# Expert tiles whose normalized rows pass through a DRAM scratch and are turned by VectorE, in place of 16 TensorE transposes per tile

## The chip, the cores and the metric

The kernel runs on one core of one Trainium2 chip. The metric is the device time of one execution in microseconds (us); the kernel before takes 2157.5 us, the median of three runs (2156.28 to 2159.11). Engines are TensorE (PE; PEld is its weight load), VectorE (DVE), ScalarE (ACT), GpSimd (POOL) and SyncE (SP), which in this kernel issues every DMA. The profile was taken of one execution.

## The reference, cut to what matters

The input `x` is (8, 512, 2048) in float32: 4096 tokens of 2048 features. The first half of the reference is an autocorrelation attention over `ctx_4096`; its result is added to `x`. The change does not touch it. The second half is a feed-forward layer of gated low-rank experts:

```python
    x = x + _L0_xattn_ref(_layernorm(x, axis=-1), ctx_4096, ctx_4096)
    x = x + _L0_ffn_ref(_layernorm(x, axis=-1), A_w, B_w, Wq_w, keys)

    # _L0_ffn_ref(x, A_w (512, 2048), B_w (2048, 512), Wq_w (16, 2048), keys (64, 16))
    q = jnp.einsum('bsd,rd->bsr', x, Wq_w)
    scores = jnp.einsum('bsr,er->bse', q, keys)
    top_vals, top_idx = jax.lax.top_k(scores, 16)
    top_w = jax.nn.softmax(top_vals, axis=-1)
    gate = jnp.sum(one_hot(top_idx, 64) * top_w[..., None], axis=-2)
    z = jnp.einsum('bsd,nd->bsn', x, A_w).reshape(..., 64, 8)
    z_gated = (z * gate[..., None]).reshape(..., 512)
    out = jnp.einsum('bsn,on->bso', z_gated, B_w) * 2.0
```

## The kernel before

The first part (to about 1350 us) runs 32 attention groups and writes their result to the output tensor in DRAM. The second part takes the 4096 tokens in 32 tiles of 128 tokens, one after another; `TT` is 32. Only this second part is changed, and mostly its tiles 4 to 31.

`each_tile` calls a function `tile_step(u, ...)` on every engine for u = 0 to 32. Step u does the products of tile u (`a`), adds the output of tile u-1 (`b`), prepares tile u+1 (`f`) and loads and sums tile u+2 (`later_tile(u)`). Steps 5 to 28 are a loop. The order of the instructions of an engine is the order in which they are written out in its `tile_step`; an engine that waits on a semaphore holds up all that stands behind it, and so does SP for the DMAs that it issues. There are four row buffers (`rows0` to `rows3`), one `xn`, one `xt`, one `xin` and one `cin`.

What happens to one tile t, with the names and lines:

- Loading (SP, in `tile_step`, L481 `cin`, L488 `xin`, L474 `rows`): the attention result of the tile, that of its mirrored partner tile, and the input, in two halves of 1024 columns. A half of `rows` is loaded once the half of the tile that used the buffer has been stored (L497, `store_half`) and has landed. A half of `cin` or `xin` is loaded once POOL has used the half before.
- Sum (POOL, L1838 `add_partner`, L1849 `add_input`): `rows` becomes attention plus input. `x2_added` counts the halves.
- Statistics (DVE, L1001 `half_statistics`, two of 512 columns per half; L1007 `tile_mean`; L1016 `invert_root`) with a square root of ACT between (L1486 `tile_root`).
- Normalizing (ACT, L1495 to L1501 `tile_scale`, four one-column instructions, then L1509 `norm_rows`): 128x2048 values from `rows` to `xn`.
- Turning (PE, L600 `turn_tile`): 16 transposes of 128x128 from `xn` into four PSUM banks `tp_ps` (the fourth is `zt_ps`), after the score product of step t-1 and ahead of its output products.
- Splitting (ACT, L1480 and L1482 `tile_high`; DVE, L995 `tile_low`): each bank is copied to `xt_full`, which lies in the same memory as `xn`, and from there into a high part, and DVE makes the low part. `tile_high` waits on the z products of the tile before, since they read `xt`.
- Queries (PE, L613 `queries`): 16 small matmuls on `xt_full` at the start of step t, copied by ACT (L1701 `copy_queries`), then the scores (PE, L830) after the z products.
- z (PE, L581 to L583 `split_mm`): 16 blocks of three matmuls with `a_hi`, `a_lo`.
- Routing (DVE, L1292 to L1301 `route`), exponentials (ACT, L1715, L1717), gate and gated z (DVE, L1305 to L1315 `gate_z`).
- Turning of the gated z in step t+1 (PE, L842 `turn_z`), split (ACT L1709 `zt_high`, DVE L1327 `zt_low`), output products (PE, `out_bank(q)`, four banks of 12 matmuls, in two PSUM banks used in turns) and the addition to `rows` (DVE, L1322 `add_out(q)`). `out_bank(q)` waits for `add_out(q-2)`.

The order on DVE in a step of the loop is `zt_low`, `route`, `tile_low` 0 and 1, `add_out(0)`, `gate_z`, `tile_low` 2, statistics of half 0, `add_out(1)`, `tile_low` 3, statistics of half 1, `tile_mean`, `add_out(2)`, `add_out(3)`, `invert_root`. On PE it is queries, `turn_z`, z, scores, `turn_tile`, four output banks.

Of the kernel before, what the change touches and what calls it, by code (L numbers as in the profile page):

```python
# [7 lines left out]
F32 = mybir.dt.float32  # L8
F32R = mybir.dt.float32r
ALU = mybir.AluOpType  # L10
ACT = mybir.ActivationFunctionType

B, L, D = 8, 512, 2048
# [120 lines left out]
def build_program(nc, x, ctx, a_w, b_w, wq_w, keys, tables, out):  # L134
# [6 lines left out]
    with ExitStack() as st:  # L141
# [13 lines left out]
        def sem(name):  # L155
            return st.enter_context(nc.semaphore(name))
# [90 lines left out]
        x2_added, stat2_step, root2_done, norm2_ready = (  # L247
            sem("x2_added"), sem("stat2_step"), sem("root2_done"), sem("norm2_ready"))
        xn_ready, tp_ready = sem("xn_ready"), sem("tp_ready")
        tp_hi, tp_lo, tp_full = sem("tp_hi"), sem("tp_lo"), sem("tp_full")  # L250
        q_ready, q_copied, sc_ready, sc_copied = sem("q_ready"), sem("q_copied"), sem("sc_ready"), sem("sc_copied")
        route_step, gate_exp, gate_step, gate_ready = (
# [36 lines left out]
        def is_step(i, n):  # L289
            return isinstance(i, int) and i == n  # L290
# [92 lines left out]
        def turned_z(u, low):  # L383

            return xt[:, low, 0:KN, :] if is_step(u, TT) else (zt_lo if low else zt_hi)[:]

        def later_tile(u):
            return not (isinstance(u, int) and u + 2 >= TT)

        def each_tile(eng, body):  # L390
            body(0, -1, 3, True, False, True)
# [12 lines left out]
        def _(sp):  # L404
# [66 lines left out]
            def load_rows(k, j, h):  # L471

                slot = j % RING
                sp.dma_start(rows[slot][:, HALVES[h]], at_tile(out_halves, RING * k + j)[:, HALVES[h]]).then_inc(rows_loaded[slot][h], 16)  # L474
# [19 lines left out]
            def store_half(u, r, h):  # L494
                sp.wait_ge(out_taken, out_at(u - 1, 2 * h + 1) + 1)
                to = at_tile(out_eighths, u - 1, 8) if h == 0 else at_tile(out_quarters, u - 1, 4)
                sp.dma_start(to[:, HALVES[h]], rows[r][:, HALVES[h]]).then_inc(out_stored, 16)  # L497
# [55 lines left out]

            steps(body)

            def tile_step(u, k, r, a, b, f):
                if later_tile(u) and not (isinstance(u, int) and u < 2):
                    sp.wait_ge(out_stored, 16 * (2 * u - 2))
                    load_rows(k, 3 + r, 1)
                if later_tile(u) and b:  # L560
                    load_others(k, 3 + r, 1)
                if later_tile(u + 1):
                    load_others(k, 4 + r, 0)
                if is_step(u, 1):
                    sp.wait_ge(stored, 16 * GROUPS)
                if is_step(u, TT):
                    store_last(r)
                elif b:
                    store_half(u, r, 0)
                    if later_tile(u + 1):  # L570
                        sp.wait_ge(out_stored, 16 * (2 * u - 1))
                        load_rows(k, 4 + r, 0)
                    store_half(u, r, 1)

            each_tile(sp, tile_step)
            sp.wait_ge(out_stored, 2 * 16 * (TT + 1))
# [2 lines left out]
        def _(pe):  # L579
# [23 lines left out]
            def queries(t, q):  # L603

                if is_step(t, 0):
                    if q == 0:
                        pe.wait_ge(small_loaded, 32)
                elif q == 0:
                    pe.wait_ge(sc_copied, t)
                    pe.wait_ge(q_copied, t)  # L610
                pe.wait_ge(tp_full, tp_at(t, q) + 1)
                for j in range(4):
                    last = nc.tensor.matmul(sc_ps[32 * j:32 * j + 32, 0:P], wq[:, 4 * q + j, :], xt_full[:, q, j, :],  # L613
                                            start=q == 0, stop=q == 3)
                last.then_inc(q_ready, 1)
# [211 lines left out]
            def tile_step(u, k, r, a, b, f):  # L827
# [4 lines left out]
                if is_step(u, 0):  # L832
                    queries(0, 2)
                    queries(0, 3)
                elif a and not is_step(u, 1):
                    for q in range(4):
                        queries(u, q)
                    pe.wait_ge(tp_lo, tp_at(u, 3) + 1)
                def turn_z(t=u):
                    pe.wait_ge(zg_ready, t)  # L840
# [50 lines left out]
                                        b_hi[:, q, m, :], b_lo[:, q, m, :], m == 0, m == KN - 1)  # L891
                    last.then_inc(out_ready, 1)

                if f and not is_step(u, 0):
                    for q in range(4):
                        turn_tile(u + 1, q)
                if b:
                    if not f:
                        pe.wait_ge(zt_hi_done, u)
                        pe.wait_ge(zt_lo_done, u)  # L900
                    for q in range(4):
                        out_bank(q)
                        if is_step(u, TT - 1) and q == 1:
                            turn_z(TT)
# [4 lines left out]
        def _(dve):  # L909
# [81 lines left out]
            def tile_low(t, q):  # L991

                dve.wait_ge(tp_hi, tp_at(t, q) + 1)
                part = slice(4 * q, 4 * q + 4)
                nc.vector.tensor_tensor(xt[:, 1, part, :], tp_ps[bank_of(t, q)][:], xt[:, 0, part, :].bitcast(F32),  # L995
                                        ALU.subtract).then_inc(tp_lo, 1)

            def half_statistics(t, slot, h):
                dve.wait_ge(x2_added, 2 * t + h + 1)
# [289 lines left out]
            def tile_step(u, k, r, a, b, f):  # L1289
# [35 lines left out]
                def zt_low(t=u):  # L1325
                    dve.wait_ge(zt_hi_done, t)
                    nc.vector.tensor_tensor(turned_z(t, 1), zt_ps[:], turned_z(t, 0).bitcast(F32), ALU.subtract).then_inc(zt_lo_done, 1)  # L1327
# [31 lines left out]
                    return  # L1359
                if not is_step(u, TT):  # L1360
                    zt_low()
                if a:
                    route()
                if f:
                    tile_low(u + 1, 0)
                    tile_low(u + 1, 1)
                add_out(0)
                if a:
                    gate_z()
                if f:  # L1370
                    tile_low(u + 1, 2)
                if later_tile(u):
                    half_statistics(u + 2, (r + 3) % RING, 0)
                add_out(1)
                if f:
                    tile_low(u + 1, 3)
                if later_tile(u):
                    half_statistics(u + 2, (r + 3) % RING, 1)
                    tile_mean(u + 2)
                if is_step(u, TT - 1):  # L1380
                    zt_low(TT)
                add_out(2)
                add_out(3)
                if later_tile(u):
                    invert_root(u + 2)

            each_tile(dve, tile_step)

        @block.scalar
        def _(act):  # L1390
# [85 lines left out]

            def tile_high(t, q):
                n = tp_at(t, q)
                act.wait_ge(tp_ready, n + 1)
                nc.scalar.activation(xt_full[:, q, :, :], tp_ps[bank_of(t, q)][:], ACT.Copy).then_inc(tp_full, 1)  # L1480
                act.wait_ge(tp_full, n + 1)
                nc.scalar.activation(xt[:, 0, 4 * q:4 * q + 4, :], xt_full[:, q, :, :], ACT.Copy).then_inc(tp_hi, 1)  # L1482
# [23 lines left out]

            def norm_rows(t, slot):
                act.wait_ge(norm2_ready, 2 * t + 2)
                nc.scalar.activation(xn[:], rows[slot][:], ACT.Identity, bias=shift2[:],  # L1509
                                     scale=rstd2[:]).then_inc(xn_ready, 1)  # L1510

            act.wait_ge(consts_set, 2)
            nc.scalar.activation(inv_sum[:, 0:1], consts[:, 1:2], ACT.Sqrt)
# [180 lines left out]
            steps(body)  # L1694

            def tile_step(u, k, r, a, b, f):
                def copy_queries():
                    act.wait_ge(q_ready, 4 * u + 4)
                    if b:
                        act.wait_ge(sc_ready, u)  # L1700
                    nc.scalar.activation(q_sb[:], sc_ps[:, 0:P], ACT.Copy).then_inc(q_copied, 1)  # L1701

                def zt_high():
# [12 lines left out]
                    act.wait_ge(route_step, 5 * u + 4)  # L1716
                    nc.scalar.activation(best_exp[:], best[:], ACT.Exp, bias=best_neg[:], accum_out=gate_sum[:]).then_inc(gate_exp, 1)  # L1717

                if a:
                    copy_queries()  # L1720
                if is_step(u, 0):
                    norm_tile(1, 1)
# [19 lines left out]
                if is_step(u, 1):  # L1742
                    zt_high()
                    norm_tile(2, 2)
                    act.wait_ge(stored, 16 * GROUPS)
                    part_high(7)
                else:
                    if f:
                        norm_tile(u + 1, (r + 2) % RING)
                    zt_high()  # L1750

                if f:
# [7 lines left out]
                    exponentials()  # L1760
                if later_tile(u):
                    tile_root(u + 2)

            each_tile(act, tile_step)

# [190 lines left out]
def laid_out(name, a):  # L1956
    if name in _INS[:2]:
        return a[:, ROWS, :]
    if name == "L0_ffn_A_w":
        return a.reshape(NFFN, 4, 4, P).transpose(1, 3, 2, 0).reshape(4, P, D)  # L1960
    if name == "L0_ffn_B_w":
        return a.reshape(4, 512, KN, P).transpose(0, 3, 2, 1).reshape(4, P, D)
    if name == "L0_ffn_Wq_w":
        wide = np.zeros((P, KD, 32), a.dtype)
        wide[:, :, :RDIM] = a.reshape(RDIM, KD, P).transpose(2, 1, 0)
        return wide.reshape(P, KD * 32)
    tall = np.zeros((4, 32, EXPERTS), a.dtype)
    tall[:, :RDIM] = a.T
    return tall.reshape(P, EXPERTS)
# [21 lines left out]
```

## Time and profile before

| What | Value |
|---|---|
| median of three runs | 2157.5 us (2156.28 to 2159.11) |
| the profiled execution, its own time | 2156.57 us |
| its span, first to last instruction | 2154.8 us |
| PE busy | 2115.7 us, 98% |
| DVE busy | 1673.8 us, 78% |
| ACT busy | 1337.5 us, 62% |
| POOL busy | 1561.3 us, 72% |
| TensorE clock granted | 1.000 of full speed |
| DMA | 287.50 MB, mean 133 GB/s |

A busy share is an average over both parts. In the slices of the page, the first part (25 of 40 slices) has DVE and POOL in the nines as well as PE. In the second part DVE stands at 4, ACT at 4 to 5, POOL at 3 to 4, the DMA engines at 4 to 5 and PE at 9. What a change of the second part is worth is read from windows and timelines there. In a timeline a row gives the start in us from the span's start, the duration in us, the engine, line and operation, what is written and read, and how many such instructions were merged.

### The profile page before, as it was taken

The page shows a single profiled execution, that of the slowest core. Times are in us where ns is not written, and L with a number is a line of the kernel's source. Part 1 is how long each engine was busy: PE and PEld are TensorE (multiplying, and loading weights), DVE is VectorE, ACT ScalarE, POOL GpSimd, SP SyncE. Part 2 cuts the span into 40 slices and gives each one's busy share as a digit, 9 for nine tenths or more (in the row PEclk, how much of TensorE's full clock was granted, in tenths as well). Part 3 has the DMA queues.
Part 4 walks back from the last instruction along what each step waited for, and adds up shares of the span by engine and source line. Part 5 has one row for each costly group of instructions (what it writes and reads, how often), then busy time and mean ns, then how long its engine had stood idle before and what let it go on. Part 6 is the DMA issues. An engine that isn't in the chain of part 4 may idle for free.

```text
span 2154.8 us, 29239 instructions
## 1 busy us (share of the span) xinstructions
PE 2115.7 (98%) x8920; PEld 1328.0 (62%) x8920; DVE 1673.8 (78%) x4051; ACT 1337.5 (62%) x3051; POOL 1561.3 (72%) x965
## 2 busy tenths in 40 slices
PE   5999999999999999999999999999999999999999
PEld 2455455455455455454454454888888888888887
DVE  7999999999999999999999999644444444444443
ACT  4786786786786786786765646644444455445441
POOL 6999999999999999999999988633343433333420
PEclk9999999999999999999999999999999999999999
DMA  7232333333333332333221246544545444444431
GB/s 282 97 108 103 120 111 103 120 111 103 121 109 103 121 109 103 122 109 103 103 89 64 83 168 239 171 158 166 175 164 174 159 166 165 158 166 172 164 119 59
DMA packets 110705, 287.50 MB, mean 133 GB/s; under 512 B 7168, under 2 KB 7296, under 8 KB 109568
## 3 DMA queue, kind: packets, MB, share of 16 engines
q1 hardware_dynamic: 110592, 286.19, 38.3%
q8 instruction: 47, 0.77, 0.1%
q14 instruction: 66, 0.54, 0.1%
HBM read 219.06 MB, written 67.11 MB: 133 GB/s over the span
## 4 chain that ended last, share of the span: by engine, by line
PE 82%; DVE 7%; POOL 6%; ACT 2%; issue 2%; DMA 1%; SPq 0%; DVEq 0%; ACTq 0%; POOLq 0%
PE pair L755 11%; PE pair L749 8%; PE out L581 6%; PE out L582 6%; PE out L583 6%; PE z L583 5%; PE z L582 5%; PE z L581 5%; PE pair L644 5%; PE evac L631 4%; PE evac L655 4%; PE evac L656 4%; PE lag L698 4%; PE pair L745 4%; PE tp L600 2%; POOL r_f L1804 2%
## 5 line engine op out<-in xcount | busy, mean ns | idle before, releaser
L1838 POOL TENSOR_TENSOR rows<-rows,cin 128x1024 f32<-128x1024 f32 x48 | 117.0, 2437 | 325.7 <-DMA rows<-out_dram 273.6
L755 PE MATMUL pair<-r_f,back 128*128 128x512 f32 x768 | 342.7, 597 | 0.5 <-DVE prod L1035 0.5
L1804 POOL TENSOR_TENSOR r_f<-prod 128x1024 f32<-128x1024 f32 x128 | 303.0, 2378 | 9.3 <-DVE prod L1033 7.4
L755 PEld LDWEIGHTS pair<-r_f,back 128*128 128x128 f32 x768 | 143.0, 190 | 192.7 <-issue 146.5
L749 PE MATMUL pair<-w_sb,wts 128*128 128x512 f32 x512 | 225.1, 592 | 1.4 <-ACT w_sb L1625 0.9
L1480 ACT ACTIVATE xn<-tp 128x512 f32<-128x512 f32 x94 | 55.1, 586 | 231.0 <-PE tp L600 230.9
L581 PE MATMUL z<-a_hi,xt 128*128 128x512 f32 x496 | 195.9, 395 | 0.0
L581 PE MATMUL out<-b_hi,zt_hi 128*128 128x512 f32 x492 | 194.3, 395 | 0.0
L583 PE MATMUL z<-a_hi,xt 128*128 128x512 f32 x496 | 193.4, 390 | 0.0
L582 PE MATMUL z<-a_lo,xt 128*128 128x512 f32 x496 | 193.3, 390 | 0.0
L582 PE MATMUL out<-b_lo,zt_hi 128*128 128x512 f32 x492 | 191.6, 389 | 0.0
L583 PE MATMUL out<-b_hi,zt_lo 128*128 128x512 f32 x492 | 191.5, 389 | 0.0
L1292 DVE COPY scores<-score_sums 128x64 f32<-128x64 f32 x32 | 7.2, 224 | 206.0 <-PE score_sums L830 206.0
L749 PEld LDWEIGHTS pair<-w_sb,wts 128*128 128x128 f32 x512 | 94.8, 190 | 108.9 <-issue 108.9
L1849 POOL TENSOR_TENSOR rows<-xin,rows 128x1024 f32<-128x1024 f32 x63 | 154.4, 2451 | 9.1 <-DMA xin<-in_x_dram 3.7
L1035 DVE TENSOR_TENSOR prod<-pair,v_cyc 128x1024 f32<-128x1024 f32 x128 | 155.2, 1212 | 0.0
L1804 POOL TENSOR_TENSOR p_f<-prod 128x1024 f32<-128x1024 f32 x64 | 151.6, 2370 | 3.9 <-DVE prod L1035 2.0
L631 PE MATMUL evac<-vf,fwd 128*128 128x512 f32 x248 | 120.3, 617 | 25.4 <-POOL vf L1864 21.2
L1563 ACT ACTIVATE e<-e,neg_max 128x512 f32<-128x512 f32 x128 | 88.6, 717 | 89.2 <-DVE pick L1098 89.1
L698 PEld LDWEIGHTS lag<-lags,p_f 128*128 128x128 f32 x1024 | 123.5, 192 | 20.5 <-issue 16.5
L1322 DVE SCALAR_TENSOR_TENSOR rows<-out,rows 128x512 f32<-128x512 f32 x127 | 86.9, 685 | 62.3 <-PE out L583 62.2
L698 PE MATMUL lag<-lags,p_f 128*128 128x128 f32 (+2 forms) x1024 | 129.0, 277 | 1.1 <-POOL p_f L1804 0.7
(234 smaller groups left out, 5576.8 us busy)
## 6 DMA issues: line engine op xcount, KB each, us to landing
out_dram<-att_sb SPq DMA_DIRECT2D x32, 1024.0 KB, 4.2
rows<-out_dram SPq DMA_DIRECT2D x64, 512.0 KB, 3.8
cin<-out_dram SPq DMA_DIRECT2D x63, 512.0 KB, 4.0
xin<-in_x_dram SPq DMA_DIRECT2D x63, 512.0 KB, 4.1
vf<-in_ctx_dram SPq DMA_DIRECT2D x31, 1024.0 KB, 5.1
out_dram<-rows SPq DMA_DIRECT2D x62, 512.0 KB, 2.8
xf<-in_x_dram SPq DMA_DIRECT2D x30, 1024.0 KB, 5.3
stat_in<-in_x_dram SPq DMA_DIRECT2D x27, 1024.0 KB, 5.1
```

The source lines that it names most:

```text
L581: nc.tensor.matmul(out, lhs_hi, rhs_hi, start=start, stop=False)
L582: nc.tensor.matmul(out, lhs_hi, rhs_lo, start=False, stop=False)
L583: return nc.tensor.matmul(out, lhs_lo, rhs_hi, start=False, stop=stop)
L631: nc.tensor.matmul(evac_ps[n % 2][:], fwd[:, n, :], v[:, fold, :], start=True, stop=True).then_inc(evac_ready, 1)
L644: last = nc.tensor.matmul(pair_ps[:, 2 * n + part, :], fwd[:, t, :], xfs[i % 2][:, fold, :], start=True, stop=True)
L698: return nc.tensor.matmul(lag_ps[t % 2][:, cols], p_f[:, row, t * P:(t + 1) * P], lags[:, cols], start=True, stop=True)
L749: last = nc.tensor.matmul(to, wts[:, 4 * blk - 4 + 2 * part + h, :], w_sb[:, 2 - 2 * part + h, :], start=h == 0, stop=h == 1)
L755: return nc.tensor.matmul(pair_ps[:, bank, :], back[:, 3 * bank + n, :], r_f[:, row, :], start=n == 0, stop=n == 2)
L1035: op = nc.vector.tensor_tensor(slot[:, 2:4, :], s_ps, vs[:, 1:3, :], ALU.mult)
L1804: nc.gpsimd.tensor_tensor(dst, prod[:, slot, 0:2, :], prod[:, slot, 2:4, :], ALU.add).then_inc(add_done, 1)
L1838: nc.gpsimd.tensor_tensor(half, first, other, op).then_inc(c_added, 1)
L1849: nc.gpsimd.tensor_tensor(half, xin2 if second else xin[:], half, ALU.add).then_inc(x2_added, 1)
```

## The change

For tiles 4 to 31 (`spread(t)`), the 16 PE transposes go. In their place, `xn` is written by `norm_rows` one step sooner (at the end of step t-2), stored whole to a DRAM scratch `turn_rows` (1 MB), loaded back by four DMAs of 32 partitions each in another arrangement (partition 32b+j holds, for the four groups c of 32 tokens, 512 features of the block b), and turned by four DVE instructions in 32x32 blocks into the four PSUM banks. The features then lie in another order over the partitions, so the weights A and Wq are laid out to match, and the first four tiles write `xn` permuted. `tile_high` waits for all four banks. On DVE, ACT and PE the order in the step changes. The output banks no longer follow `turn_tile`; the queries of tile u+1 stand ahead of the last output bank of step u.

```diff
+        def ahead(u):
+            return later_tile(u) and spread(u + 2)
...
+            def store_turn(t):
+                sp.wait_ge(xn_half, t - FIRST_SPREAD + 1)
+                sp.dma_start(turn_rows, xn[:]).then_inc(turn_stored, 16)
+
+            def load_turn(t):
+                sp.wait_ge(turn_stored, 16 * (t - FIRST_SPREAD + 1))
+                from_rows = turn_rows.rearrange("(c j) (b f) -> b j c f", c=4, b=4)
+                to = xn[:].rearrange("p (c f) -> p c f", c=4)
+                for b in range(4):
+                    sp.dma_start(to[SPREAD * b:SPREAD * (b + 1)], from_rows[b]).then_inc(turn_loaded, 16)
...  SP, in tile_step
                         load_rows(k, 4 + r, 0)
+                    if ahead(u):
+                        store_turn(u + 2)
                     store_half(u, r, 1)
+                    if ahead(u):
+                        load_turn(u + 2)
...  PE
                 elif a and not is_step(u, 1):
-                    for q in range(4):
-                        queries(u, q)
+                    if is_step(u, 2):
+                        for q in range(4):
+                            queries(u, q)
                     pe.wait_ge(tp_lo, tp_at(u, 3) + 1)
...
-                if f and not is_step(u, 0):
+                if f and not (is_step(u, 0) or spread(u + 1)):
                     for q in range(4):
                         turn_tile(u + 1, q)
...
                     for q in range(4):
+                        if q == 3 and f and not is_step(u, 1):
+                            for part in range(4):
+                                queries(u + 1, part)
                         out_bank(q)
...  DVE
+            def turn_spread(t, q):
+                if q == 0:
+                    dve.wait_ge(turn_loaded, 64 * (t - FIRST_SPREAD + 1))
+                if q == 3:
+                    dve.wait_ge(zt_lo_done, t - 1)
+                by_block = xn[:].rearrange("p (c q m i) -> p q m c i", c=4, q=4, m=4)[:, q]
+                nc.vector.transpose(tp_ps[q][:].rearrange("p m (c j) -> p m c j", c=4), by_block).then_inc(tp_ready, 1)
...
                     zt_low()
+                if f and spread(u + 1):
+                    for q in range(4):
+                        turn_spread(u + 1, q)
+                if later_tile(u):
+                    half_statistics(u + 2, (r + 3) % RING, 0)
                 if a:
                     route()
                 if f:
                     tile_low(u + 1, 0)
+                add_out(0)
+                if f:
                     tile_low(u + 1, 1)
-                add_out(0)
-                if a:
-                    gate_z()
-                if f:
-                    tile_low(u + 1, 2)
-                if later_tile(u):
-                    half_statistics(u + 2, (r + 3) % RING, 0)
-                add_out(1)
-                if f:
-                    tile_low(u + 1, 3)
                 if later_tile(u):
                     half_statistics(u + 2, (r + 3) % RING, 1)
                     tile_mean(u + 2)
+                if a:
+                    gate_z()
+                add_out(1)
+                if f:
+                    tile_low(u + 1, 2)
+                    tile_low(u + 1, 3)
...
                 add_out(2)
-                add_out(3)
                 if later_tile(u):
                     invert_root(u + 2)
+                add_out(3)
...  ACT
-                act.wait_ge(tp_ready, n + 1)
+                act.wait_ge(tp_ready, n + 4 - q if spread(t) else n + 1)
...
+                if spread(t):
+                    nc.scalar.activation(xn[:], rows[slot][:], ACT.Identity, bias=shift2[:], scale=rstd2[:]).then_inc(xn_half, 1)
...
-                    if f:
-                        norm_tile(u + 1, (r + 2) % RING)
+                    if is_step(u, 2):
+                        norm_tile(3, 3)
                     zt_high()
...  ACT, at the end of tile_step
                     tile_root(u + 2)
+                    if ahead(u):
+                        tile_scale(u + 2)
+                if f and not is_step(u, 1):
+                    copy_queries(u + 1)
+                if ahead(u):
+                    norm_rows(u + 2, (r + 3) % RING)
```

## Rows read from the trace of the kernel before

**Rows 1.** Busy time by windows: us, busy us and instructions, clock, DMA share, GB/s.
```profile
1610.00:2100.00 490.00, 490.00 (x2895) 407.71 (x2892) 216.70 (x666) 232.22 (x406) 181.90 (x76) 1.00 0.47 161
```

**Rows 2.** Timeline of PE, one step of the loop (the split matmuls merged out).
```profile
1672.05 0.33 PE L830 MATMUL score_sums<-keys,q_sb 128*128 128x64 f32 x2
1672.21 1.48 PE L600 MATMUL tp<-ident,xn 128*128 128x128 f32 x12
...
1673.88 0.48 PE L581 MATMUL out<-b_hi,zt_hi 128*128 128x512 f32 x1
...
1684.96 1.08 PE L613 MATMUL score_sums<-xn,wq 128*32 128x128 f32 x32
...
1686.38 0.48 PE L581 MATMUL z<-a_hi,xt 128*128 128x512 f32 x1
...
1697.37 0.33 PE L830 MATMUL score_sums<-keys,q_sb 128*128 128x64 f32 x2
```

**Rows 3.** Timeline of DVE in the same step.
```profile
1672.41 0.23 DVE L1292 COPY scores<-score_sums 128x64 f32<-128x64 f32 x1 [6.76 <-PE score_sums L830]
...
1673.67 0.21 DVE L1301 MATCH_REPLACE8 rest<-best,rest 128x64 f32<-128x64 f32 x1
...
1677.51 0.15 DVE L1305 RECIPROCAL gate_inv<-gate_sum 128x1 f32<-128x1 f32 x1
...
1678.95 0.68 DVE L995 TENSOR_TENSOR xt<-tp,xt 128x512 fp32r<-128x512 f32 x1
1679.55 1.27 DVE L1001 BATCH_NORM_STATS2 bn_x<-rows 128x6 f32<-128x512 f32 x2
1680.74 0.67 DVE L1322 SCALAR_TENSOR_TENSOR rows<-out,rows 128x512 f32<-128x512 f32 x1
...
1681.93 1.27 DVE L1001 BATCH_NORM_STATS2 bn_x<-rows 128x6 f32<-128x512 f32 x2
...
1683.74 0.68 DVE L1322 SCALAR_TENSOR_TENSOR rows<-out,rows 128x512 f32<-128x512 f32 x1
1685.67 0.15 DVE L1016 RECIPROCAL norm_x<-norm_x 128x1 f32<-128x1 f32 x1
```

**Rows 4.** Timeline of ACT in the same step.
```profile
1672.86 0.60 ACT L1480 ACTIVATE xn<-tp 128x512 f32<-128x512 f32 x1 [7.92 <-PE tp L600]
...
1678.28 0.58 ACT L1480 ACTIVATE xn<-zt 128x512 f32<-128x512 f32 x1
...
1686.10 0.28 ACT L1701 ACTIVATE q_sb<-score_sums 128x128 f32<-128x128 f32 x1 [2.17 <-PE score_sums L613]
1686.28 0.29 ACT L1495 ACTIVATE norm_x<-norm_x 128x1 f32<-128x1 f32 x1
...
1687.67 2.10 ACT L1509 ACTIVATE xn<-rows,shift,rstd 128x2048 f32<-128x2048 f32 x1
```

**Rows 5.** DMA issues of the whole run: count, KB each, median us from issue to landing.
```profile
out_dram<-att_sb SPq DMA_DIRECT2D x32, 1024.0 KB, 4.2
rows<-out_dram SPq DMA_DIRECT2D x64, 512.0 KB, 3.8
...
vf<-in_ctx_dram SPq DMA_DIRECT2D x31, 1024.0 KB, 5.1
...
v_last<-in_ctx_dram SPq DMA_DIRECT2D x32, 256.0 KB, 4.9
...
wq<-in_L_ffn_Wq_w_dram SPq DMA_DIRECT2D x1, 256.0 KB, 3.7
```

**Rows 6.** Timeline of SP: DMAs issued one behind another, with no wait between.
```profile
1328.38 0.43 SPq L544 DMA_DIRECT2D keys<-in_L_ffn_keys_dram  x1
1328.85 0.43 SPq L469 DMA_DIRECT2D b_in<-in_L_ffn_B_w_dram  x1
```

**Rows 7.** Timeline of POOL: the sums of half 1 of one tile.
```profile
1695.45 2.39 POOL L1838 TENSOR_TENSOR rows<-rows,cin 128x1024 f32<-128x1024 f32 x1 [2.37 <-DMA cin<-out_dram]
1697.92 2.39 POOL L1849 TENSOR_TENSOR rows<-xin,rows 128x1024 f32<-128x1024 f32 x1
```

More of the change, by code:

```diff
@@ L249, in build_program @@
         xn_ready, tp_ready = sem("xn_ready"), sem("tp_ready")
+        xn_half = sem("xn_half")
+        turn_stored, turn_loaded = sem("turn_stored"), sem("turn_loaded")
+        turn_rows = nc.dram_tensor("turn_rows", (P, D), F32, kind="Internal").ap()
         tp_hi, tp_lo, tp_full = sem("tp_hi"), sem("tp_lo"), sem("tp_full")
@@ L385, in turned_z, with spread @@
             return xt[:, low, 0:KN, :] if is_step(u, TT) else (zt_lo if low else zt_hi)[:]
+        FIRST_SPREAD = 4
+        SPREAD = P // 4
+        def spread(t):
+            return not (isinstance(t, int) and t < FIRST_SPREAD)
         def later_tile(u):
             return not (isinstance(u, int) and u + 2 >= TT)
+        def ahead(u):
+            return later_tile(u) and spread(u + 2)
         def each_tile(eng, body):
@@ L897, in tile_step @@
                 if b:
-                    if not f:
+                    if not f or spread(u + 1):
                         pe.wait_ge(zt_hi_done, u)
@@ L1508, in norm_rows @@
                 act.wait_ge(norm2_ready, 2 * t + 2)
-                nc.scalar.activation(xn[:], rows[slot][:], ACT.Identity, bias=shift2[:],
-                                     scale=rstd2[:]).then_inc(xn_ready, 1)
+                if spread(t):
+                    nc.scalar.activation(xn[:], rows[slot][:], ACT.Identity, bias=shift2[:], scale=rstd2[:]).then_inc(xn_half, 1)
+                else:
+                    nc.scalar.activation(xn[:].rearrange("p (k b i) -> p b k i", b=4, k=KD),
+                                         rows[slot][:].rearrange("p (b k i) -> p b k i", b=4, k=KD),
+                                         ACT.Identity, bias=shift2[:], scale=rstd2[:]).then_inc(xn_ready, 1)
             act.wait_ge(consts_set, 2)
@@ L1696, in tile_step, with copy_queries @@
             def tile_step(u, k, r, a, b, f):
[L1697 to L1700, printed above, removed]
+                def copy_queries(t=u):
+                    act.wait_ge(q_ready, 4 * t + 4)
+                    if not is_step(t, 0):
+                        act.wait_ge(sc_ready, t)
                     nc.scalar.activation(q_sb[:], sc_ps[:, 0:P], ACT.Copy).then_inc(q_copied, 1)
@@ L1717, in exponentials @@
                     nc.scalar.activation(best_exp[:], best[:], ACT.Exp, bias=best_neg[:], accum_out=gate_sum[:]).then_inc(gate_exp, 1)
-                if a:
+                if is_step(u, 0) or is_step(u, 1) or is_step(u, 2):
                     copy_queries()
@@ L1959, in laid_out @@
     if name == "L0_ffn_A_w":
-        return a.reshape(NFFN, 4, 4, P).transpose(1, 3, 2, 0).reshape(4, P, D)
+        return a.reshape(NFFN, 4, 4, 4, P // 4).transpose(2, 1, 4, 3, 0).reshape(4, P, D)
     if name == "L0_ffn_B_w":
@@ L1964, in laid_out @@
         wide = np.zeros((P, KD, 32), a.dtype)
-        wide[:, :, :RDIM] = a.reshape(RDIM, KD, P).transpose(2, 1, 0)
+        wide[:, :, :RDIM] = a.reshape(RDIM, 4, KD, P // 4).transpose(1, 3, 2, 0).reshape(P, KD, RDIM)
         return wide.reshape(P, KD * 32)
```

## The prediction

> **What bounds the kernel now.** Only the second part of the kernel is changed, so I looked first at the busy times by windows there. In the 490 us from 1610 to 2100 PE is busy all 490, DVE 217, ACT 232, POOL 182, and the DMA engines 47% at 161 GB/s [rows 1]: PE alone bounds this part, at full clock. Then I read the timeline of PE for one step. Step starts are taken at the score product: it comes at 1672.05 and again at 1697.37, so a tile costs 25.3 us. In that time stand the score product (0.16), the 16 transposes (1672.21 to 1673.88, 1.67), the 48 output matmuls (to 1684.96, 11.1), queries and `turn_z` (to 1686.38, 1.4) and the 48 z matmuls (to 1697.37, 11.0) [rows 2]. The timelines of DVE and ACT in the same step then give durations and show where these engines wait for PE.
>
> **What the change takes from PE.** The 1.67 us of transposes go in steps 3 to 30, 28 of them. The queries only move; between two output banks they add a change of kind of matmul, and the first matmul after such a change starts the next about 0.1 us later, so I count 1.6 us per tile. If PE stayed the bound, the period would be 23.7 us and the gain 28 x 1.6 = 45 us.
>
> **What it adds is a loop that does not pass through PE.** There is one `xn`. In one step it is loaded in the new arrangement, turned by DVE, overwritten by `tile_high`, read by the queries, overwritten by `norm_rows` for the next tile, stored and loaded again. The period can't be shorter than the way from one landing of the turned load to the next. I call the landing L and follow what each engine has in order behind it, in us after L. DVE has nothing to do out of order: `route`, the statistics and the additions all stand behind `turn_spread`, which waits for L.
>
> - `turn_spread`, four DVE instructions of 128x512 from SBUF to PSUM. The trace has no such instruction. All its DVE passes over 128x512 take 0.60 each when back to back (L995 at 1678.95, next at 1679.55) [rows 3], and I take that: 2.4, and 0.1 to start, 2.5. From below nothing in the trace is quicker. From above I allow 1.2 each, since a pass that turns could go at half the rate.
> - `half_statistics` of half 0: 1679.55 to 1680.74, 1.2. `route`: 1672.41 to 1673.88, 1.5. So `route` ends at 5.2.
> - `tile_low` 0, `add_out(0)`, `tile_low` 1: the stretch 1680.74 to 1681.93 holds one addition and one `tile_low`, 0.6 each: 1.8, to 7.0.
> - statistics of half 1 and mean: 1681.93 to 1683.74, 1.8, to 8.8. `gate_z`: 1677.51 to 1678.95, 1.4, to 10.2.
> - `add_out(1)`, `tile_low` 2 and 3, `add_out(2)`: 4 x 0.6 = 2.4, to 12.6. `invert_root` (0.15) and the hop to ACT: 0.3, to 12.9. All [rows 3].
> - ACT: `tile_scale` 1686.28 to 1687.67, 1.4; `copy_queries` moves ahead of the rows and takes 0.2; `norm_rows` 2.1 [rows 4]. To 16.6. (`tile_high` needs 1672.86 to 1678.86, 6.0 us, for its four copies [rows 4]; started at 2.5 it is done at 8.5, beside DVE's work, and holds up nothing here.)
> - Store of 1 MB to DRAM: the stores of `att_sb`, also 1 MB, land after 4.2 [rows 5]. With 0.1 of hop, 20.9.
> - Load, four DMAs of 256 KB. SP needs 0.47 from one issue to the next without waits [rows 6], so the fourth goes out 1.4 after the first. The bounds: a single 1 MB load in 2 KB pieces lands after 5.1 (`vf`), and 1.4 + 3.7 (`wq`, 256 KB) gives the same; the other 256 KB load, `v_last`, needs 4.9, and 1.4 + 4.9 = 6.3 [rows 5]. The upper end: 512 KB and 1 MB differ by 1.3 us [rows 5], so 2.6 of the 5.1 are bytes; at half the rate the load needs 5.1 + 2.6 = 7.7. I take 6.3, since 256 KB pieces with their own completion are what is loaded, and the 32-fold row is the better known of the two. With a hop: 27.3.
>
> So the loop takes 27.3 where the period before was 25.3.
>
> A second way round the same loop is as long. SP issues the second half of `rows`, `cin` and `xin` of the next tile behind the four loads, and these wait for the store. In the new order everything of SP up to the next step stands behind a store that can't be issued before `norm_rows` ends. Their data come behind the turned data: 6.3 + 2 x 1.3 = 8.9 after the store landed; POOL then needs 1695.45 to 1700.3, 4.9 [rows 7], to 13.8; the statistics of half 1 wait for it, and from there to the landed store are 1.8 + 1.4 + 2.4 + 0.3 + 1.4 + 0.2 + 2.1 + 4.3 = 13.9. Together 27.7. I take the longer one, 27.7.
>
> PE meanwhile is led by DVE: output bank 2 waits for `add_out(0)` (L + 6.4) and bank 3 for `add_out(1)` (L + 10.8); from there one bank (2.75), `turn_z` (0.4) and z (11.0) put the next score product at L + 25.1, so PE arrives at every step ahead of its load and then waits for it.
>
> **Sum.** From the landing for tile 4 to that for tile 31 there are 27 periods: 27 x (27.7 - 25.3) = 65 us. Lead-in and end: the first load comes 1 us or so after the score product of step 3, and step 30, with no statistics in it, is 1.5 shorter; these cancel. `norm_rows` in another order of writing for four tiles is covered (2.1 on ACT, whose wait of 7.9 us for PE [rows 4] stands behind it). The extra 2 MB of traffic per tile bring 4 MB to 6 MB and the rate from 161 [rows 1] to about 220 GB/s; the DMA engines have room. So 2156.6 + 65 = 2221.6 for the profiled execution, which lies 0.9 below the median of the runs; I say 2220.
>
> **A rule that speaks against the load.** Each of the four loads writes 32 partitions only, and no row shows such a DMA. By it the load would be near the upper end, 7.7, and the period 29.1. No trace here tells.
>
> The page "VectorE: DVE Perf Modes", section "The three transpose paths", gives 311 ns for a 128x128 bf16 transpose of VectorE; an estimate from that page of four such per bank is 1.24 us, close to my upper end of 1.2 for `turn_spread`.
>
> **Rivals.**
>
> 1. The load goes at full rate, 5.1. Both ways round the loop shorten by 1.2, to 26.5: 27 x 1.2 = 32, 2189 us. For it: all wide loads of the trace. Against: four narrow ones.
> 2. The load goes at half rate, 7.7: both ways are 1.4 longer, 29.1: 27 x 3.8 = 103, 2260 us. For it: how narrow the loads are; against: nothing in the trace, which has no narrow ones.
> 3. The turns take 1.2 each. The DVE way grows by 2.4 to 29.7: 27 x 4.4 = 119, 2276 us. Against: each DVE pass of the trace goes at 0.60, copies and statistics alike.
> 4. Faster: the loop stays under the old period, and PE's 1.6 us are kept. The place is the round trip through DRAM, store plus load. The rest of the loop is 16.6, with hops 16.8, so the round trip decides: above 8.5 us the kernel is slower, at 6.9 it would be 45 us faster, 2112. For it: PE is at 100% and DVE at 44% in this part, and an engine that is idle for half the time looks able to take 2.4 us more. Against: the quickest 1 MB load and store of the trace add up to 9.3. It needs the store and load to be quicker by 0.8, or DVE's order to let part of it lie beside.
>
> **How the numbers follow.** The forecast has 0.40; its own range, for a period between 27.0 and 28.4, is 2200 to 2240. Full rate 0.17, half rate 0.20, slow turns 0.08, faster 0.12, and 0.03 for a loop that ends at the old period. What this kernel's measurement can tell from no change is 0.2%, 4.3 us. The range from 2172 to 2278 reaches over rivals 1 to 3 and leaves out the faster case and no change (0.15) and a little above. Faster 0.12, same 0.03, slower 0.85.
>
> **What the profile of the changed kernel would show.** The `L600` transposes for tile 4 and up are gone, and the first DVE turn of each step waits for a DMA into `xn` for some us (before, DVE waited there for the scores). PE has idle time ahead of output banks 2 and 3, released by `add_out` (DVE on `rows`), about 4 us per tile in all. The period of the score product is 27.7. The store lands 4.2 after its issue, the last load 6.3 after the first load's issue. A turn takes 0.6. POOL's sum of half 1 waits for `cin` until after the turned load. I would be wrong if DVE never waits for the load, if PE has no gaps ahead of banks 2 and 3 (then the order, not the round trip, was what I misjudged), or if a turn is far from 0.6.

## The result, and the profile after

The changed kernel takes 2258.0 us (median of four runs, 2254.7 to 2258.6) against 2158.2 us for the kernel before (median of four, 2156.3 to 2159.1): ratio 1.046, 95% interval 1.0442 to 1.0479. It is 100 us slower. The sign and the place were forecast, the size was not: the likeliest case said 2220 us, and the time is that of rival 2, a load at half rate, 2260 us, which had a chance of 0.20.

The windows of the kernel after, in the stretch of [rows 1] (us, then busy us and instructions of PE, PEld, DVE, ACT, POOL, then clock, DMA share, GB/s):

```profile
1610.00:2100.00 490.00, 435.82 (x2319) 346.39 (x2318) 233.32 (x668) 202.91 (x359) 161.82 (x68) 0.94 0.68 219
```

PE no longer fills the stretch: 54 us of 490 are idle. DMA went from 161 to 219 GB/s, as the extra 2 MB per tile ask. The timeline of PE for one step, the counterpart of [rows 2], shows where the idle time is:

```profile
1768.92 0.33 PE L860 MATMUL score_sums<-keys,q_sb 128*128 128x64 f32 x2
1769.06 0.48 PE L611 MATMUL out<-b_hi,zt_hi 128*128 128x512 f32 x1
...
1774.40 0.39 PE L613 MATMUL out<-b_hi,zt_lo 128*128 128x512 f32 x1
1778.34 0.50 PE L611 MATMUL out<-b_hi,zt_hi 128*128 128x512 f32 x1 [3.55 <-DVE rows L1365]
...
1781.28 1.08 PE L643 MATMUL score_sums<-xn,wq 128*32 128x128 f32 x32
1783.29 0.50 PE L611 MATMUL out<-b_hi,zt_hi 128*128 128x512 f32 x1 [0.92 <-DVE rows L1365]
...
1786.16 0.60 PE L873 MATMUL zt<-ident,zg 128*128 128x128 f32 x4
...
1797.53 0.33 PE L860 MATMUL score_sums<-keys,q_sb 128*128 128x64 f32 x2
```

In this step 28.6 us pass from score product to score product, where they were 25.3. The transposes are gone; PE waits 3.55 ahead of output bank 2 and 0.92 ahead of bank 3, both for an `add_out` of DVE. Over the stretch its idle time is 54 us in 16.9 steps, 3.2 per step. What holds DVE up is the first turn of each step. Timeline of DVE, one step (the counterpart of [rows 3]), and the last turn of the run beside the first:

```profile
1420.36 1.91 DVE L1039 STREAM_TRANSPOSE tp<-xn 128x512 f32<-128x512 f32 x3 [10.54 <-DMA xn<-turn_rows]
...
1742.92 1.91 DVE L1039 STREAM_TRANSPOSE tp<-xn 128x512 f32<-128x512 f32 x3 [10.77 <-DMA xn<-turn_rows]
1744.74 0.68 DVE L1039 STREAM_TRANSPOSE zt<-xn 128x512 f32<-128x512 f32 x1
1745.34 1.24 DVE L1044 BATCH_NORM_STATS2 bn_x<-rows 128x6 f32<-128x512 f32 x2
1746.50 0.20 DVE L1335 COPY scores<-score_sums 128x64 f32<-128x64 f32 x1
...
1750.38 1.28 DVE L1044 BATCH_NORM_STATS2 bn_x<-rows 128x6 f32<-128x512 f32 x2 [0.64 <-POOL rows L1905]
...
1752.20 0.15 DVE L1348 RECIPROCAL gate_inv<-gate_sum 128x1 f32<-128x1 f32 x1
...
1756.03 0.15 DVE L1059 RECIPROCAL norm_x<-norm_x 128x1 f32<-128x1 f32 x1
...
2204.75 1.91 DVE L1039 STREAM_TRANSPOSE tp<-xn 128x512 f32<-128x512 f32 x3 [10.70 <-DMA xn<-turn_rows]
```

In each step shown DVE sits idle for 10.5 to 10.8 us until the turned rows land. From 1420.36 to 2204.75 are 27 periods, 29.05 us each on the mean: the step of the kernel before is 25.33 on the mean of its score products, and 27 x (29.05 - 25.33) = 100 us, all of the loss. The round trip, in the timeline of SP, and the sums of POOL (the counterparts of [rows 6, 7]):

```profile
1728.37 0.33 SPq L487 DMA_DIRECT2D rows<-out_dram  x1
1730.97 0.33 SPq L572 DMA_DIRECT2D turn_rows<-xn  x1
1731.58 0.36 SPq L510 DMA_DIRECT2D out_dram<-rows  x1
1735.06 1.77 SPq L580 DMA_DIRECT2D xn<-turn_rows  x4
1737.10 0.36 SPq L487 DMA_DIRECT2D rows<-out_dram  x1
1737.72 0.36 SPq L494 DMA_DIRECT2D cin<-out_dram  x1
...
1759.76 0.33 SPq L572 DMA_DIRECT2D turn_rows<-xn  x1
```

```profile
1745.53 2.37 POOL L1894 TENSOR_TENSOR rows<-rows,cin 128x1024 f32<-128x1024 f32 x1 [8.14 <-DMA cin<-out_dram]
1747.98 2.36 POOL L1905 TENSOR_TENSOR rows<-xin,rows 128x1024 f32<-128x1024 f32 x1
```

The store goes out at 1730.97, the first load 4.1 later, and DVE starts on the landed rows at 1742.92, 7.9 after that. The next store goes out at 1759.76, 16.8 later. POOL's first sum waits for `cin`, issued at 1737.72 behind the four loads, and DVE's statistics wait 0.64 for POOL: the second way round was, as forecast, a little the longer. The page's DMA rows, to be read with [rows 5]:

```profile
rows<-out_dram SPq DMA_DIRECT2D x64, 512.0 KB, 6.0
cin<-out_dram SPq DMA_DIRECT2D x63, 512.0 KB, 5.7
...
turn_rows<-xn SPq DMA_DIRECT2D x28, 1024.0 KB, 4.0
```

### The profile page after: what moved, and what is told of

Its sections match the earlier page's. It is cut to its first block, busy times and chain, and to the rows that moved or that the text cites. A ratio compares the mean times of both kernels' runs of the same rounds, so it can differ in the third digit from the quotient of the medians.

```text
span 2256.3 us, 28655 instructions
## 1 busy us (share of the span) xinstructions
PE 2120.2 (94%) x8472; PEld 1306.2 (58%) x8472; DVE 1735.3 (77%) x4163; ACT 1334.1 (59%) x3051; POOL 1560.5 (69%) x965
## 4 chain that ended last, share of the span: by engine, by line
PE 42%; DMA 15%; DVE 14%; POOL 13%; ACT 6%; issue 6%; SPq 3%; DVEq 0%; POOLq 0%; ACTq 0%
DMA cin<-out_dram 9%; PE pair L785 9%; PE pair L779 7%; DMA turn_rows<-xn 5%; PE pair L674 4%; PE evac L661 4%; PE evac L685 3%; PE evac L686 3%; PE lag L728 3%; PE pair L775 3%; POOL rows L1905 3%; ACT xn L1556 3%; POOL r_f L1860 2%; POOL rows L1894 2%; SPq L580 2%
## 5 line engine op out<-in xcount | busy, mean ns | idle before, releaser
L611 PE MATMUL out<-b_hi,zt_hi 128*128 128x512 f32 x492 | 217.6, 442 | 96.8 <-DVE rows L1365 96.8
L1039 DVE STREAM_TRANSPOSE tp<-xn 128x512 f32<-128x512 f32 x84 | 53.5, 698 | 309.2 <-DMA xn<-turn_rows 309.2
L612 PE MATMUL out<-b_lo,zt_hi 128*128 128x512 f32 x492 | 207.8, 422 | 0.0
L613 PE MATMUL out<-b_hi,zt_lo 128*128 128x512 f32 x492 | 207.2, 421 | 0.0
L611 PEld LDWEIGHTS out<-b_hi,zt_hi 128*128 128x128 f32 x492 | 101.6, 207 | 134.6 <-DVE rows L1365 110.3
```

The costliest lines, as they stand in the source:

```text
L611: nc.tensor.matmul(out, lhs_hi, rhs_hi, start=start, stop=False)
L612: nc.tensor.matmul(out, lhs_hi, rhs_lo, start=False, stop=False)
L613: return nc.tensor.matmul(out, lhs_lo, rhs_hi, start=False, stop=stop)
```

## The experiments

All are edits of the changed kernel; in the edits shown, `...` marks lines that are left out. The table gives, as medians over the 27 steps from the first turn of the run to the last, from the timelines of SP and DVE: a, from the first turn of a step to the next store's issue; b, from the store's issue to SP's first load; c, from that load's issue to the first turn. The period is the mean of the 27 steps, so a few long ones can put it above a + b + c. In the run without stores a ends at the load. c is the time of the load only where DVE waits for the load, which holds in all runs but the last of the table.

| Kernel | a | b | c | period | us (median) |
|---|---|---|---|---|---|
| changed kernel | 16.8 | 4.0 | 7.9 | 29.05 | 2258.0 |
| wide load | 16.9 | 4.0 | 6.2 | 27.3 | 2207.3 |
| no store | 16.7 | - | 9.6 | 26.1 | 2178.3 |
| two queues | 16.8 | 4.0 | 7.1 | 28.0 | 2233.9 |
| narrow loads, nothing behind | 20.1 | 4.0 | 7.8 | 32.0 | 2335.1 |
| wide load, nothing behind | 20.1 | 4.0 | 5.6 | 29.85 | 2280.0 |
| more PE work | 16.8 | 4.0 | 7.9 | 28.9 | 2256.9 |
| earlier root | 15.0 | 6.1 | 7.9 | 29.2 | 2261.3 |
| earlier root, store first | 14.9 | 4.9 | 9.2 | 28.9 | 2253.0 |
| other order, two queues | 15.1 | 4.5 | 7.1 | 26.9 | 2196.9 |
| the same, in halves | 14.5 | 3.4 | 8.8 | 27.1 | 2204.8 |
| other order, two queues, store first | 15.1 | 4.9 | 8.5 | 28.5 | 2242.9 |

In the halves, a ends at and b runs from the first half's store.

**Wide load** (rows land in the wrong order for the turn).

```diff
-                from_rows = turn_rows.rearrange("(c j) (b f) -> b j c f", c=4, b=4)
+                from_rows = turn_rows.rearrange("(c x) (b f) -> (x b) c f", c=4, b=4)
                 to = xn[:].rearrange("p (c f) -> p c f", c=4)
-                for b in range(4):
-                    sp.dma_start(to[SPREAD * b:SPREAD * (b + 1)], from_rows[b]).then_inc(turn_loaded, 16)
+                sp.dma_start(to, from_rows).then_inc(turn_loaded, 16)
...  DVE, in turn_spread
-                    dve.wait_ge(turn_loaded, 64 * (t - FIRST_SPREAD + 1))
+                    dve.wait_ge(turn_loaded, 16 * (t - FIRST_SPREAD + 1))
```

> One DMA of 128 partitions loads the scratch back, with the same 1 MB in the same 2 KB pieces; the pieces come to other partitions than the turn needs, so the rows are in the wrong order. Theory (the loop through DRAM sets the period, and the load is slow because each of its four DMAs writes only 32 partitions): the load falls from 7.9 to about 5.1 us, both ways round the loop shorten by about 2.7 us, 27 x 2.7 = 73 us, so 2185 us. Rival A (the load is slow because of its 2 KB pieces from a scratch just written, or because of the other loads beside it): 7.9 stays, 2258 us. Rival B (PE or its lower clock sets the period): no change, 2258 us.

Measured 2207.3 us, ratio to before 1.0225 (1.0208 to 1.0242). The same bytes in the same pieces over 128 partitions land 1.7 us sooner: 27 x 1.7 = 46 of the 51 us gained. Neither rival's 2258 us came. But the load took 6.2, not 5.1, so the width is not the whole of it. And two things changed at once, the width and the number of DMAs (one in place of four); the next two runs tell them apart.

**Nothing behind the loads**, narrow and wide. SP waits for `turn_loaded` before it issues the second half of `rows`, `cin` and `xin`. The edit is that of the narrow loads; with the wide one the count is 16.

```diff
+                if later_tile(u) and not (isinstance(u, int) and u < 3):
+                    sp.wait_ge(turn_loaded, 64 * (u - 2))
                 if later_tile(u) and not (isinstance(u, int) and u < 2):
                     sp.wait_ge(out_stored, 16 * (2 * u - 2))
```

> SP issues the second half of rows, cin and xin only once the turned rows have landed, so the four narrow loads have nothing behind them; the way through POOL gets longer, so the time rises (2300 us or more); the number wanted is the load. Wide loads with traffic behind them took 6.2 us where a 1 MB load of the kernel before takes 5.1. Theory (1.1 us of the load is what is issued behind it, the rest is the narrowness): 6.8 us. Rival (the narrowness is the whole of it): 7.9 us.

> The same wait with the one load of 128 partitions (rows in the wrong order for the turn). Theory (what is issued behind costs it 1.1 us): 5.1 us in place of 6.2. Rival (reading the scratch just written costs it): 6.2 us.

Alone, the narrow loads need 7.8 and the wide one 5.6, 2.2 less. What is issued behind costs the wide load 0.6 and the narrow ones 0.1, so the expected 6.8 is missed (its rival, 7.9, came), and the 5.6 lies between theory and rival. The way through POOL grew, a rose to 20.1, and the time with it (2335 and 2280 us), one run each.

The windows of these two runs, while the bytes of the turned rows move and no other DMA of the program is in flight, tell width from number (narrow, then wide; the last two numbers are the DMA share and GB/s):

```profile
1734.50:1736.00 1.50, 1.50 (x8) 1.25 (x7) 0.00 (x0) 0.00 (x0) 0.00 (x0) 1.00 1.06 217
1748.00:1749.50 1.50, 1.50 (x8) 1.26 (x7) 0.00 (x0) 0.00 (x0) 0.00 (x0) 1.00 1.05 408
```

In both the DMA engines are busy throughout, and the narrow loads move 217 GB/s where the wide one moves 408. The four had been issued from 1730.58 to 1732.35, before this stretch. 1 MB (1.05 million bytes) takes 4.8 us at 217 GB/s and 2.6 at 408, and the difference is the 2.2 us: it is the width, and the four issues cost nothing that shows.

**Two queues.** SP loads blocks 0 and 1, ACT blocks 2 and 3:

```diff
...  SP, in load_turn
-                for b in range(4):
+                for b in (0, 1):
...  ACT
                     norm_rows(u + 2, (r + 3) % RING)
+                    act.wait_ge(turn_stored, 16 * (u + 2 - FIRST_SPREAD + 1))
...
+                    for b in (2, 3):
+                        nc.scalar.dma_start(to[SPREAD * b:SPREAD * (b + 1)], from_rows[b]).then_inc(turn_loaded, 16)
```

> The loads of partitions 0 to 63 are issued by SP, those of 64 to 127 by ACT, so the two halves are in flight at once from two queues. Theory (each half is held up by what its 32 or 64 partitions take, and the other half can go beside it): the load takes 5.5 to 6 us in place of 7.9, 2195 to 2210 us. Rival (the DMA engines work off one DMA after another whatever queue it is on, as the Trainium skill, page SBUF — State Buffer, section on issuing two DMAs for both halves, states with +6%): 2240 to 2258 us.

Measured 2233.9 us, 1.0354 (1.0337 to 1.0372). The load fell by 0.8 of 7.9 and the period by 1.0, and the gain is 24 us. It lies between the two and nearer the rival: the halves go beside each other at most in small part. Not even that much is shown, since the last of the four loads also goes out about 0.9 us sooner, and this run does not tell that from the halves going side by side.

**No store** after the first (the loads bring old rows).

```diff
             def store_turn(t):
...
+                if is_step(t, FIRST_SPREAD):
+                    sp.wait_ge(xn_half, 1)
+                    sp.dma_start(turn_rows, xn[:]).then_inc(turn_stored, 16)
+
+            def load_turn(t):
...
                 sp.wait_ge(xn_half, t - FIRST_SPREAD + 1)
...
-                sp.wait_ge(turn_stored, 16 * (t - FIRST_SPREAD + 1))
+                sp.wait_ge(turn_stored, 16)
```

> Only the first spread tile is stored; the later loads start as soon as norm_rows ends and bring the old rows. Theory (loop): the 4.1 us of the store leave both ways round the loop, 27 x 4.1 = 111 us, 2147 us, a little below the kernel before, period about 24.9; the load stays at 7.9. Rival (the period is set by PE, its clock, or by DMA bandwidth and not by the round trip's latency): a loss of traffic alone, 2230 us or more.

Measured 2178.3 us, 1.0093 (1.0077 to 1.011). Most of the store's time is gained, less what the load grew, which is why the expected 2147 us is missed. On the mean of the steps the store had taken 4.3, and the load rose from 8.0 to 9.3: 27 x (4.3 - 1.3) = 81, against 80 us measured. The load now starts 1.5 us behind the 512 KB store of the output and 2.5 behind the load of `rows`, which it had been held clear of by the wait. The timeline of SP there:

```profile
1724.49 0.33 SPq L487 DMA_DIRECT2D rows<-out_dram  x1
1725.53 0.35 SPq L510 DMA_DIRECT2D out_dram<-rows  x1
1726.99 2.02 SPq L582 DMA_DIRECT2D xn<-turn_rows  x4
```

**PE turns, new orders.** `spread` returns False, and ACT normalizes tile u+1 at the start of each step as before.

> The changed orders of DVE, PE and ACT are kept (queries ahead of the last bank, statistics sooner, copy of the queries at the end of the step), but every tile is turned by the 16 PE transposes and nothing goes through DRAM. Theory (only the round trip costs): PE is the bound again, period 25.3 to 25.5, 2157 to 2163 us. Rival (the new orders themselves cost a good part): 2180 us or more.

Measured 2161.0 us over ten runs, 1.0016 (1.0006 to 1.0026). PE is busy for all 490 us of the stretch again. The orders by themselves cost about 4 us; the other 97 come with the way through DRAM and the turns on DVE.

**More PE work.**

```diff
                 if b and not (is_step(u, 1) or is_step(u, TT)):
+                    pe.wait_ge(zg_ready, u)
+                    for _ in range(4):
+                        for m in range(KN):
+                            nc.tensor.transpose(zt_ps[:, m, :], zg[:, m * P:(m + 1) * P], ident[:])
                     turn_z()
```

> The changed kernel with turn_z done five times in place of once in steps 2 to 31 (16 more 128x128 transposes of PE each, about 1.7 us, of the same data into the same bank, so the work that the change took from PE is put back as such). Theory (PE waits for the loop): PE reaches output banks 2 and 3 later and waits less, 2258 us, at most 2263. Rival (PE at its lower clock is part of what bounds): 28 x 1.7 = 48 us more, 2300 us.

Measured 2256.9 us, 1.0466 (1.0449 to 1.0484): as many transposes as the change removed, put back, cost nothing. Once the loop binds, what PE saves is worth nothing.

**Earlier root**: `invert_root(u + 2)` right behind `add_out(1)` on DVE.

> On DVE, invert_root of tile u+2 stands right behind add_out(1), ahead of tile_low 2 and 3 and add_out(2). Nothing else changes. Theory (the loop's length is the sum of what stands in order on DVE and ACT and of the round trip): three DVE passes of 0.6 leave both ways round, 27 x 1.8 = 49 us, 2209 us. Rival (only the DMA traffic or PE sets the period): 2250 to 2258 us.

Measured 2261.3 us, 1.0482 (1.0461 to 1.0503): no gain, against my theory as I had put it. The way behind the landing did fall by 1.8. The store took it back:

```profile
1704.01 0.33 SPq L487 DMA_DIRECT2D rows<-out_dram  x1
1704.80 0.33 SPq L572 DMA_DIRECT2D turn_rows<-xn  x1
1705.47 0.35 SPq L510 DMA_DIRECT2D out_dram<-rows  x1
1710.95 1.75 SPq L580 DMA_DIRECT2D xn<-turn_rows  x4
```

The store goes out 0.8 us behind a load of 512 KB and needs 6.1 (6.15 in this step). In the changed kernel that load had left 2.6 us before (1728.37 to 1730.97) and was over when the store began. So I turned the two round:

```diff
                     store_half(u, r, 0)
+                    if ahead(u):
+                        store_turn(u + 2)
                     if later_tile(u + 1):
                         sp.wait_ge(out_stored, 16 * (2 * u - 1))
                         load_rows(k, 4 + r, 0)
-                    if ahead(u):
-                        store_turn(u + 2)
```

> The earlier invert_root again, and SP issues the store of the normalized rows ahead of the load of the first half of rows, not behind it. With the earlier root alone, the way behind the landing did fall from 16.8 to 15.0 us, but the store came 0.8 to 1.2 us behind that load of 512 KB and took 6.1 in place of 4.0. Theory (the store's data wait behind the load's in the same queue, and that gave the 1.8 us back): the store lands after 4.0 to 4.3, period 27.2, 2205 to 2215 us. Rival (something else holds the period at 29, such as POOL's sums): the store gets quicker and another wait takes its place, 2245 us or more.

Measured 2253.0 us, 1.0451 (1.0434 to 1.0469). The store fell to 4.9, and the load rose from 7.9 to 9.2:

```profile
1725.70 0.33 SPq L572 DMA_DIRECT2D turn_rows<-xn  x1
1726.21 0.34 SPq L487 DMA_DIRECT2D rows<-out_dram  x1
1726.83 0.81 SPq L510 DMA_DIRECT2D out_dram<-rows  x1
1730.57 1.78 SPq L580 DMA_DIRECT2D xn<-turn_rows  x4
```

Now 512 KB of `rows` and 512 KB of output lie between store and load. The expected 2210 is missed, and the rival, by which something else holds the period, is not right either. In the stretch from 1610 to 2100 DVE waits 12.2 us per step for the load and 0.4 for POOL's sums (10.7 and 0.5 in the changed kernel), so the round trip still holds it. The same traffic lies around the round trip in either order.

**Towards a version that beats the kernel before.** On DVE: statistics of half 0 ahead of `turn_spread`, `gate_z` and `add_out(1)` ahead of the statistics of half 1, then `tile_low(2)`, `invert_root`, `tile_low(3)`, `add_out` 2 and 3; two queues for the loads.

> Two queues for the loads (SP partitions 0 to 63, ACT 64 to 127) and another order on DVE: statistics of half 0 ahead of turn_spread, gate_z and add_out(1) ahead of the statistics of half 1, then tile_low 2, invert_root, tile_low 3, add_out 2 and 3. Theory (loop): behind the landing DVE has 2.5 + 1.5 + 1.8 + 1.4 + 0.6 + 1.8 + 0.6 + 0.3 = 10.5 in place of 12.9; with ACT 3.7, store 4.1 and the load at 7.0 the way through DVE is 25.3, that through POOL shorter, so about 2157 us, the time before. Rival (the way through POOL stays the longer one, since rows, cin and xin still start behind the store): 26.5 or more, 2190 us.

Measured 2196.9 us, 1.0179 (1.0162 to 1.0196), the best of those that turn the right rows by way of DRAM. The way to the store is 15.1, not 14.2, for one wait that I had not counted: `gate_z` comes sooner than ACT's exponentials.

```profile
1725.54 0.16 DVE L1348 RECIPROCAL gate_inv<-gate_sum 128x1 f32<-128x1 f32 x1 [1.22 <-ACT best_exp L1768]
```

The same, with `norm_rows`, store and loads in two column halves, and 4 KB per partition more to land in:

> As the run with the other order, and norm_rows, the store and the loads in two column halves: the first half is stored while ACT normalizes the second, and SP loads partitions 0 to 63 once the first is stored; the pieces that would overwrite unstored columns land in a buffer of 4 KB per partition, so there are eight loads and eight turns of half the size (about 0.4 us more on DVE). Theory (loop): first loads start 1.05 + 2.8 us after norm_rows starts in place of 6.2, the last land about 1.5 us sooner; period 24.2 to 24.8, 2130 to 2145 us, below the kernel before. Rival (eight narrow loads of 128 KB cost more in issue and landing than the overlap gives): 25.5 or more, 2160 us or more.

Measured 2204.8 us, 1.0224 (1.0207 to 1.0241). The rival holds, where 2130 to 2145 was expected: the first store came 0.6 sooner and took 1.1 less, and c rose from 7.1 to 8.8. In c now lies also that ACT's loads, of the second half of the columns, wait for the second store.

And the other order with two queues again, whole, and with the store first:

> The other order on DVE and the two queues again (2197 us, period 26.9: 15.1 to the store, 4.6 store, 7.1 load), with the store ahead of the load of rows. Theory: the store falls to 4.0, its longer cases too, period 26.2 to 26.4, 2178 to 2185 us: the best of the versions through DRAM, and still above the kernel before, since 15.1 + 4.0 + 7.1 is over 25.3. Rival (rows come later and POOL or DVE waits for them): 2197 us or more.

Measured 2242.9 us, 1.0400 (1.0383 to 1.0418), 46 us worse than without, as its rival had it: `rows` land later, and POOL and with it DVE wait. The waits of DVE from 1610 to 2100 (in all, times, longest):

```profile
DVE bn_x L1044 <- POOL rows L1911: 76.5, 17, 5.0
DVE tp L1039 <- DMA xn<-turn_rows: 3.8, 6, 1.1
```

The statistics of half 0, which in this order stand ahead of the turns, are held 4.5 us per step for POOL's sum, and the load is nearly always there by then. So the 8.5 of the table is not the load's time here, and the way through POOL holds the period. No version that I ran beats the kernel before.

## Why the prediction was right and wrong

- **PE bounds, and 1.6 us per tile go from it.** Right for PE, and worth nothing: more PE work left the time where it was.
- **A loop that does not pass through PE.** Right. From the landing to the next store I had 16.6 (and a hop), measured 16.8, of which 0.5 is DVE's wait for POOL: the terms by themselves came out at 16.3. Four turns took 2.4, 0.60 each back to back, as the other DVE passes, so rival 3 fell. This is also where the Trainium skill's 311 ns for a 128x128 bf16 transpose ("VectorE: DVE Perf Modes", "The three transpose paths") would have misled, taken times four: a 128x512 in float32 is at 0.60, not 1.24.
- **Store 4.2.** Measured 4.0 on the median and 4.3 on the mean; in the first five steps after the lead-in it was 4.5 to 6.6.
- **Load 6.3: the step that failed.** It is 7.9. I chose the value by a 256 KB load and left the upper end, 7.7, worked out as half rate, to a rival. With it the two ways were 28.7 and 29.1; measured 29.05. The loads alone (7.8 narrow, 5.6 wide, at 217 and 408 GB/s) show that it is their width. The rule of the Trainium skill on this, "SBUF — State Buffer", section "Door 1: The DMA port swizzle", agrees with the trace: half the rate for 32 partitions, 217 against 408 GB/s. The statement that two DMAs on different halves run one after the other stands in the page's section "Can I just issue two DMAs to hit both halves?". It agrees roughly: two queues won 0.8 of 7.9 us, 10%, where the page has 6%, and part of the 0.8 may be the earlier issue.
- **The way through POOL is the longer.** Right: `cin` held POOL 8 us per step, and DVE waited 0.5 for POOL. Its data took from 1735.06 to 1745.53, 10.5 us; I had 8.9, short by the load's 1.6.
- **PE's idle time ahead of banks 2 and 3, about 4 us.** Measured 3.55 + 0.92 in the step shown, 3.2 on the mean of the stretch.
- **Faster, if the round trip were under 8.5.** It is 11.9. Without the store it is 9.3 on the mean, and the kernel is still 0.9% slower.
- **Not foreseen**: a DMA's time depends on what was issued just ahead of it. The store took 4.0 us with a 512 KB load 2.6 ahead of it, and 6.1 with that load 0.8 ahead. Taking 1.8 us out of the engines' part moved the store into the wake of a load, and the period stayed. A loop with a DMA in it is not a sum of fixed terms. What remains open is how much of the first steps' longer stores comes from the same neighbour; I did not try it apart. Nor do the runs tell whether it is the shared queue or the shared DMA engines that make neighbours slow.

## What to carry to other kernels

When work moves off the bounding engine on to others, write down the loop it makes from one use of its buffer to the next, with each in-order engine and each landing in it, and compare that length with the period; busy shares of 44% on DVE say nothing about it. A DMA into 32 partitions is to be priced at half rate, 217 against 408 GB/s here, even where four of them together fill all 128. And when a loop is bound by round trips, look at what is issued just ahead of each: shortening another term may only move the DMA behind it.

## What the runs showed of the hardware

The granted clock of PE fell shortly after some of its waits, not after all. In the stretch above it is 0.94 on the mean. In the changed kernel from 1720 to 1730, behind a wait of 1.96 us, it is 0.83:

```profile
1720.00:1730.00 10.00, 9.36 (x63) 7.17 (x64) 7.39 (x20) 7.45 (x16) 1.55 (x1) 0.83 0.51 170
```

and PE's timeline there:

```profile
1720.64 0.50 PE L611 MATMUL out<-b_hi,zt_hi 128*128 128x512 f32 x1 [1.96 <-DVE rows L1365]
...
1721.44 0.40 PE L611 MATMUL out<-b_hi,zt_hi 128*128 128x512 f32 x1
1721.68 0.42 PE L612 MATMUL out<-b_lo,zt_hi 128*128 128x512 f32 x1
1721.90 0.62 PE L613 MATMUL out<-b_hi,zt_lo 128*128 128x512 f32 x1
1722.32 0.63 PE L611 MATMUL out<-b_hi,zt_hi 128*128 128x512 f32 x1
```

PE resumed at one matmul in 0.23 us, the higher of its two levels (1.2 and 2.4 GHz), and from 1721.9 to 1724.5 went at 0.43, the lower one. Two steps on, behind the waits of 3.55 and 0.92 us shown above, it stayed at 0.23. With 1.7 us more of transposes per tile the clock of the stretch from 1610 to 2100 is 0.99, and the time is the same (2256.9 against 2258.0), so no cost of the lower clock shows here: PE stood idle for 3.2 us per step on the mean.
